# A gated two-layer network on one core: the third main group's routing moved forward in feed-forward 4, the first expert block put inside the last attention's entry, and one shared product moved back

## The chip, the cores and the metric

The kernel runs on one core of a Trainium2 chip. The core has a matrix engine (TensorE, PE in the profile), a vector engine (VectorE, DVE), an activation engine (ScalarE, ACT), GpSimd (POOL), and SyncE (SP), which here only issues transfers. Each engine runs its own queue in order and meets the others at semaphores. The metric is the device time of one execution in microseconds; several executions are taken and their median is given.

## The reference, cut to what matters

x has 16 sequences of 128 tokens of 256 numbers. Four steps are added to it one after the other, each behind a gate:

```
x += tanh(g0) * wkv(layernorm(x), ctx)           # a recurrence over time
x += tanh(g1) * (mlp(layernorm(x)) + experts512)  # feed-forward with 1024 hidden, plus top-8 of 512 tiny experts
x += tanh(g2) * linear_attention(layernorm(x), ctx)
x += tanh(g3) * moe(layernorm(x))
# moe: scores = sigmoid(x @ gate); the two best of 8 experts by scores + bias
for e in range(8):
    out += mask_e * (silu(rin @ w1[e].T) * (rin @ w3[e].T)) @ w2[e].T   # rin = chosen rows, scaled
out = scatter_add(out) + (silu(x @ sw1.T) * (x @ sw3.T)) @ sw2.T        # the shared expert
```

Everything is float32 with the precision that three matmul passes on split operands give in the big products.

## The kernel before, in words

The 16 sequences are four **main groups** of four (0 to 3). Each passes through the recurrence, the feed-forward with its 12 units (eight of the MLP, four of the 512 tiny experts), the attention, and the expert layer. One schedule, written out by hand, sets the order for all engines: `START`, then for each of the four feed-forwards its parts 1 to 13 with the items of `PLAN` behind each part, then `LAST`. Every engine walks the same list (`SCHED`) and issues its own share of each item, so an item's place in the list is its place in each engine's queue. In this text "feed-forward 4" is `("mlp", 3)`.

A part u of a feed-forward issues unit u-1's up products and the down product of unit u-4 (`LAG` is 3). Six banks (`ring`) hold results of TensorE; a bank is opened again once the engine that reads it has freed it.

The expert layer of a main group g is made of these items:

- `moe_in g 0, 1, 2`: part 0 is the statistics on VectorE (L1179 to L1186) and the power that gives 1/sigma on GpSimd (L1601); part 1 the normalisation on VectorE (L1201, writes `xn`); part 2 the transposes on TensorE (L631) and the copy to `xt_f` on ScalarE (L1063). `attn_in` has the same three parts, but ends with a split into a high part `ax_h` (ScalarE, L1059) and a low part `ax_l` (VectorE, L1349).
- `moe g 0`: router scores (TensorE L904), then the choice of two experts per token on VectorE (L1436 to L1458). `moe g 1`: the shared expert's up products (L913, L1106, L1466).
- `place g 0, 1, 2`: counts per expert by a matmul (L923), then the slot of each row on VectorE (L1485 to L1509), then the bookkeeping of which expert owns which block of 128 rows (L1514 to L1529).
- `rows g t`: ScalarE scales tile t twice into buffers (L1118, L1119). `send g t`: GpSimd scatters them into the sorted table `x_rows` in HBM (L1637). It waits for the slots of the group and for the scaled row.
- `load 0 n` and `blk 0 n`: SyncE loads pair n of blocks of the sorted table (L1681); groups 0 to 2 share a first table of 31 blocks, and loads from it start when all their sends have landed. On TensorE `blk n` transposes pair n (L683), does the up products of pair n-1 (L699, after reading the expert numbers into registers), the transposes of the hidden rows of n-2 (L709), and the down products of n-3 (L718). On ScalarE it copies and applies silu (L1131, L1139, L1148, L1156). On VectorE it copies the home indices (L1534) and multiplies (L1543). GpSimd scatters the results of pair n-3 into `y_rows` (L1645).
- `shared g 0`: the shared expert's down product, eight matmuls (L672); `shared g 1`: its addition to x (L1205).
- At the end `fetch`, `gather`, `fetch_tile`, `gather_tile` bring the expert results back and store x.

The loop on VectorE for the home indices reads:

```python
elif kind == "blk":
    for n in range(part + (part > 0), min(part + 2, PAIRS)):
        dve.wait_ge(blocks_loaded[n % 4], 16 * (n // 4 + 1))
        dve.tensor_copy(block_home[:, n, 0:pair_blocks(n)].unsqueeze(2), ...
```

Of the kernel before, what the change touches and what calls it, by code (L numbers as in the profile page):

```python
# [117 lines left out]
def steps(text):  # L118

    out = []  # L120
    for item in text.split(","):
        kind, g, *which = item.split()
        out += [(kind, int(g), int(part)) for part in which]
    return out
# [68 lines left out]
    },  # L193
}

LAST = """mlp_out 3 0, attn_in 3 0, shared 0 0 1, shared 1 0, shared 2 0, attn_in 3 1, shared 1 1, shared 2 1,
    attn_in 3 2, blk 0 0 1, attn 3 0 1 2 3, blk 0 2, attn 3 4 5 6 7, blk 0 3, attn 3 8, blk 0 4, attn 3 9 10, moe_in 3 0,
    blk 0 5, moe_in 3 1, blk 0 6, moe_in 3 2, blk 0 7, moe 3 0, blk 0 8, rows 3 12 13, place 3 0 1, rows 3 14,
    rows 3 15, send 3 12 13 14 15, blk 0 9, place 3 2, blk 0 10 11 12 13 14 15 16 17 18 19 20,
    fetch 0 0 1 2 3 4 5, blk 0 21, gather 0 0, blk 0 22, gather 0 1, blk 0 23, gather 0 2, blk 0 24, gather 0 3, blk 0 25,  # L200
    gather 0 4 5, blk 0 26, moe 3 1, shared 3 0 1, fetch_tile 1 0 1 2 3, gather_tile 1 0 1 2 3"""

# [1 line left out]
for f in range(NG):  # L204

    for part in range(1, MLP_UNITS + 2):
# [5 lines left out]
        if part in PLAN[("mlp", f)]:  # L212
            SCHED += steps(PLAN[("mlp", f)][part])
SCHED += steps(LAST)

# [1610 lines left out]
```

How the kernel before makes its waits and increments, by code:

```python
        def full(eng, key):  # L501
            k, n = place[key]
            eng.wait_ge(bank_full[k], n)
            return ring[k]
# [1 line left out]
        def freed(eng, key):  # L507
            k, n = place[key]
            eng.wait_ge(bank_free[k], n)
# [1 line left out]
        def weigh_values(eng, g, c):  # L512
            ee_a, v = ee_a_of[g], v_of[g]
            eng.wait_ge(ctx_loaded[g], 16 * C)
            freed(eng, (("wkv_in", g), "T", c))
            va = ee_a[c][:, :, :].rearrange("p s (t j) -> p s t j", t=GT)[:, :, :, 1:]
            return eng.tensor_tensor(va[:, 0], va[:, 1], v[c][:, :].rearrange("p (t j) -> p t j", t=GT), ALU.mult)
# [36 lines left out]
        def hidden_made(eng, n):  # L555
            kind, f, u = ALL_UNITS[n]
            if ALL_UNITS[n] in HID_TURN:
                eng.wait_ge(hid_ready, HID_TURN[ALL_UNITS[n]])
            else:
                freed(eng, ((kind, f), "B", u))
# [1 line left out]
        def sent(eng, grp):  # L563
            for k in range(SENDS):
                done = sum(1 for g in range(GROUPS[grp][-1] + 1) for n in range(2 * GT) if (g * 2 * GT + n) % SENDS == k)
                eng.wait_ge(row_sent[k], 16 * done)
# [1 line left out]
        def y_done(eng, n):  # L569
            for k in range(RESULTS):
                blocks = sum(pair_blocks(m) for m in range(k, n, RESULTS))
                if blocks:
                    eng.wait_ge(y_sent[k], 16 * blocks)
# [20 lines left out]
        def xt_wait(eng, n):  # L595
            if n > 0:
                k, turn = place[last_xt_read[n - 1]]
                eng.wait_ge(bank_full[k], turn)
```

## Time and profile before

| | |
|---|---|
| time, median of 3 runs | 522.52 us (520.04 to 523.59) |
| the profiled execution, span from first to last instruction | 517.5 us (its time with what lies around the span isn't listed apart) |
| TensorE busy | 449.8 us, 87% |
| VectorE busy | 360.9 us, 70% |
| ScalarE busy | 246.7 us, 48% |
| GpSimd busy | 154.5 us, 30% |
| mean granted clock of TensorE | 0.967 |

Busy time is a sum over the whole span. Matmuls are pipelined and their ends are modelled, so that starts are the better mark. A granted clock of 1.00 is 2.4 GHz, one of 0.50 is 1.2 GHz. Times in the rows are microseconds from the start of the span.

### The profile page before, as it was taken

Reading aid. Unit: us, or ns where it says so; the run is one execution under the profiler, and the core shown is the slowest. Engines: PE = TensorE matmul, PEld = TensorE weight load, DVE = VectorE, ACT = ScalarE, POOL = GpSimd, SP = SyncE. Lnnn points to the kernel's source line nnn. Section 1 sums busy time; section 2 is a strip of 40 time slices with the busy share of each in tenths; the row PEclk is TensorE's granted clock in tenths of the full one; section 3 lists DMA queues with packets and bytes.
Section 4 is the critical chain, followed back from the end, with each engine's and each line's share of the span. In section 5 each row is a group of like instructions: output and inputs, shape, how many; then the busy total and the mean of one; then the engine's idle time right before and its main releaser. Section 6 shows DMA issues by size and latency. Waiting matters only on the chain. (4 is left out here: it accounts for less than half of the span.)

```text
span 517.5 us, 7233 instructions
## 1 busy us (share of the span) xinstructions
PE 449.8 (87%) x2142; PEld 355.1 (69%) x2142; DVE 360.9 (70%) x1034; ACT 246.7 (48%) x452; POOL 154.5 (30%) x156
## 2 busy tenths in 40 slices
PE   1617999599999889999999999898999799899991
PEld 1315688368578666878778886787777588788851
DVE  6896779995289986565987966978867554531173
ACT  3618574363576346346125315470453454955540
POOL 3955342330002131110000001032336014477771
PEclk9966999799999989999999999999999999999997
DMA  8500312000300000960000000123232423346394
GB/s 303 187 31 30 103 31 83 0 1 0 101 2 0 2 0 14 310 178 0 1 1 1 1 0 2 32 71 102 90 115 83 123 73 91 114 139 208 85 385 153
DMA packets 32965, 42.00 MB, mean 81 GB/s; under 512 B 3483, under 2 KB 26781, under 8 KB 32928
## 3 DMA queue, kind: packets, MB, share of 16 engines
q1 hardware_dynamic: 28224, 32.28, 20.7%
q0 software_dynamic: 3744, 8.42, 4.4%
q10 hardware_dynamic: 960, 0.86, 0.5%
q8 instruction: 18, 0.29, 0.2%
q14 instruction: 19, 0.16, 0.1%
HBM read 24.97 MB, written 18.39 MB: 84 GB/s over the span
## 5 line engine op out<-in xcount | busy, mean ns | idle before, releaser
L660 PE MATMUL acc<-w_down,act_s 128*128 128x256 f32 x384 | 92.2, 387 | 0.9 <-DVE act_s L1386 0.9
L660 PEld LDWEIGHTS acc<-w_down,act_s 128*128 128x128 f32 x384 | 74.6, 195 | 13.2 <-DVE act_s L1386 1.3
L636 PE MATMUL ring<-xt_h,up_l 128*128 128x512 f32 x160 | 70.5, 441 | 2.9 <-DVE xt_l L1356 1.5
L1601 POOL TENSOR_TENSOR rstd<-var_eps,minus_half 128x4 f32<-128x4 f32 x14 | 14.9, 1068 | 176.5 <-DVE var_eps L1186 176.5
L637 PE MATMUL ring<-xt_l,up_h 128*128 128x512 f32 x160 | 63.8, 399 | 0.0
L638 PE MATMUL ring<-xt_h,up_h 128*128 128x512 f32 x160 | 63.7, 398 | 0.0
L1098 ACT ACTIVATE act_s<-ring 128x512 f32<-128x512 f32 x48 | 28.6, 597 | 59.9 <-PE ring L638 59.6
L631 PE MATMUL ring<-small,xn 128*128 128x128 f32 x160 | 23.6, 297 | 26.2 <-ACT xn L998 14.1
L699 PE MATMUL ring<-up_e,act_s 128*128 x184 | 44.3, 383 | 2.3 <-issue 2.0
L1637 POOL DMA_INDIRECT x_rows<-main_a,slots x32 | 31.1, 971 | 43.7 <-ACT main_a L1119 34.8
L1390 DVE TENSOR_TENSOR act_s<-ring,act_s 128x512 f32<-128x512 f32 x32 | 22.0, 686 | 30.8 <-PE ring L638 21.0
L631 PEld LDWEIGHTS ring<-small,xn 128*128 128x128 f32 x160 | 20.1, 153 | 29.6 <-ACT xn L998 14.9
L699 PEld LDWEIGHTS ring<-up_e,act_s 128*128 128x128 f32 x184 | 33.1, 190 | 7.1 <-issue 3.5
L636 PEld LDWEIGHTS ring<-xt_h,up_l 128*128 128x128 f32 x160 | 30.5, 191 | 10.5 <-DVE xt_l L1356 1.8
L638 PEld LDWEIGHTS ring<-xt_h,up_h 128*128 128x128 f32 x160 | 30.5, 191 | 7.3
L637 PEld LDWEIGHTS ring<-xt_l,up_h 128*128 128x128 f32 x160 | 30.6, 191 | 7.0 <-issue 1.4
L1098 ACT ACT_TABLE_LOAD x21 | 26.9, 1283 | 0.4
L1205 DVE SCALAR_TENSOR_TENSOR x_nat<-ring,small,x_nat 128x512 f32<-128x512 f32 x24 | 18.0, 749 | 11.2 <-PE ring L893 7.7
L1179 DVE BATCH_NORM_STATS2 stats<-x_nat 128x6 f32<-128x256 f32 x64 | 22.4, 413 | 4.7 <-DMA x_nat<-in_x 4.3
L1645 POOL DMA_INDIRECT y_rows<-act_s,block_home x16 | 15.9, 994 | 30.3 <-ACT act_s L1156 25.6
L726 PE MATMUL ring<-exps_t_l,sel_exps 128*128 128x512 f32 x24 | 13.5, 564 | 9.9 <-DVE exps_t_l L1361 5.3
L1543 DVE TENSOR_TENSOR pairs<-ring,pairs 128x256 f32<-128x256 f32 x12 | 5.1, 423 | 23.3 <-ACT pairs L1139 23.3
(275 smaller groups left out, 987.8 us busy)
## 6 DMA issues: line engine op xcount, KB each, us to landing
main_b<-x_rows SPq DMA_DIRECT2D x22, 257.0 KB, 2.8
x_rows<-v_t SPq DMA_DIRECT2D x1, 3983.5 KB, 16.7
up_l<-y_rows SPq DMA_DIRECT2D x5, 512.0 KB, 7.0
stage<-in_w_mlp SPq DMA_DIRECT2D x8, 256.0 KB, 2.6
up_e<-in_w_moe SPq DMA_DIRECT2D x8, 256.0 KB, 2.6
x_rows<-v_t SPq DMA_DIRECT2D x1, 1927.5 KB, 22.8
x_nat<-in_x SPq DMA_DIRECT2D x7, 256.0 KB, 7.7
out_x<-x_nat SPq DMA_DIRECT2D x6, 256.0 KB, 5.2
```

Source lines behind the costliest of these rows:

```text
L631: last = pe.transpose(bank[:, t * P:(t + 1) * P], xn[n % 2][:, t, c * P:(c + 1) * P], ident)
L636: pe.matmul(out, wl, xh, start=first, stop=False, skip_group_check=True)
L637: pe.matmul(out, wh, xl, start=False, stop=False, skip_group_check=True)
L638: return pe.matmul(out, wh, xh, start=False, stop=final, skip_group_check=True)
L660: last = pe.matmul(acc[t // 2][:, t % 2, :], act_s[n % RING][:, tok], w_down[:, u, :], start=u == 0 and t % 2 == 0, stop=final, skip_group ...
L699: last = pe.matmul(bank[:, j * 2 * P:(j + 1) * 2 * P], x_block_t[n % 2][:, c, j * P:(j + 1) * P], up_e[:, bass.ds(e * UP + c * 2 * P, 2 * ...
L1098: act.activation(act_s[n % RING][:, :], bank[:, :], ACT.Silu).then_inc(free_sem((step, "A", u)), 1)
L1179: last = dve.bn_stats(stats[:, n, t, :], x_nat[:, b, :])
L1205: return dve.scalar_tensor_tensor(out, bank, gates[:, gate:gate + 1], out, ALU.mult, ALU.add)
L1390: free((step, "B", u), dve.tensor_tensor(s[:, :], bank[:, :], s[:, :], ALU.mult))
L1637: pool.indirect_dma_start(x_rows[group_of(g)], bass.IndirectOffsetOnAxis(ap=slots[:, t, k:k + 1], axis=0), to_send[n % SENDS], None).then_ ...
L1645: pool.indirect_dma_start(y_rows, bass.IndirectOffsetOnAxis(ap=block_home[:, n, j:j + 1], axis=0), y_blocks[n % RESULTS][:, j * D:(j + 1) ...
```

## The change

Only the order of items in the schedule changes; the work is the same. In feed-forward 4 the second and third part of `moe_in 2`, the router and shared up products of group 2 (`moe 2 0 1`) each stand one part earlier; `place 2` stays in part 11, now ahead of the first rows; rows and sends of group 2 are spread over parts 11 and 12 and none are left for part 13. In `LAST`, `blk 0 0` comes between the first and second part of `attn_in 3`, and `shared 2 0` and `shared 2 1` move from there to the place around `blk 0 9`.

```diff
-        8: "attn 2 10, peer_in 3 0, moe_in 2 0, rows 1 4 5, send 1 4 5",
-        9: "moe_in 2 1, rows 1 6, send 1 6",
-        10: "moe_in 2 2, rows 1 7, send 1 7",
-        11: "moe 2 0 1, place 2 0 1 2",
-        12: "rows 2 8 9 10, send 2 8 9 10",
-        13: "mlp 3 14 15, rows 2 11, send 2 11, load 0 0 1 2",
+        8: "attn 2 10, peer_in 3 0, moe_in 2 0, rows 1 4 5, send 1 4 5, moe_in 2 1",
+        9: "moe_in 2 2, rows 1 6, send 1 6",
+        10: "moe 2 0 1, rows 1 7, send 1 7",
+        11: "place 2 0 1 2, rows 2 8 9, send 2 8 9",
+        12: "rows 2 10 11, send 2 10 11",
+        13: "load 0 0 1 2, mlp 3 14 15",
...
-LAST = """mlp_out 3 0, attn_in 3 0, shared 0 0 1, shared 1 0, shared 2 0, attn_in 3 1, shared 1 1, shared 2 1,
-    attn_in 3 2, blk 0 0 1, attn 3 0 1 2 3, blk 0 2, attn 3 4 5 6 7, blk 0 3, attn 3 8, blk 0 4, attn 3 9 10, moe_in 3 0,
+LAST = """mlp_out 3 0, attn_in 3 0, shared 0 0 1, shared 1 0, blk 0 0, attn_in 3 1, shared 1 1, attn_in 3 2, blk 0 1,
+    attn 3 0 1 2 3, blk 0 2, attn 3 4 5 6 7, blk 0 3, attn 3 8, blk 0 4, attn 3 9 10, moe_in 3 0,
...
-    rows 3 15, send 3 12 13 14 15, blk 0 9, place 3 2, blk 0 10 11 12 13 14 15 16 17 18 19 20,
+    rows 3 15, send 3 12 13 14 15, shared 2 0, blk 0 9, place 3 2, shared 2 1, blk 0 10 11 12 13 14 15 16 17 18 19 20,
```

## Rows read from the trace of the kernel before

**Rows 1.** Windows: us, busy PE, PEld, DVE, ACT, POOL (instructions), clock, DMA share, GB/s.
```profile
400.00:410.00 10.00, 6.48 (x35) 4.95 (x34) 7.12 (x16) 3.17 (x6) 0.62 (x1) 1.00 0.53 159
```

**Rows 2.** Waits of TensorE, 396 to 412 us: total us, times, longest.
```profile
PE ring L631 <- DVE xn L1201: 1.2, 1, 1.2
PE ring L699 <- issue: 1.1, 1, 1.1
PE ring L683 <- DMA main_b<-x_rows: 0.9, 1, 0.9
```

**Rows 3.** Chain of waits, 384 to 412 us: start, us, what.
```profile
398.11 2.68 DMA x_rows<-main_a,slots
...
401.92 3.37 DMA main_b<-x_rows
```

**Rows 4.** Timeline, TensorE, 360 to 396: start, us, line, tiles, count [idle before].
```profile
368.90 1.89 PE L660 MATMUL acc<-w_down,act_s 128*128 128x256 f32 x8
...
374.45 1.04 PE L631 MATMUL ring<-small,xn 128*128 128x128 f32 x8
...
380.84 3.68 PE L913 MATMUL ring<-xt_f_pad,stage 128*128 128x512 f32 x8
384.66 0.41 PE L923 MATMUL ring<-wanted,later 128*128 128x32 f32 x2
...
393.99 1.99 PE L660 MATMUL acc<-w_down,act_s 128*128 128x256 f32 x8 [0.86 <-DVE act_s L1386]
```

**Rows 5.** Timeline, VectorE, 368 to 389 us.
```profile
369.33 0.17 DVE L1186 TENSOR_SCALAR var_eps<-mv 128x4 f32<-128x4 f32 x1
...
372.18 1.38 DVE L1201 TENSOR_SCALAR xn<-x_nat,mv,rstd 128x256 f32<-128x256 f32 x4
...
384.44 0.17 DVE L1458 SCALAR_TENSOR_TENSOR row_bias<-row_scale,mv 128x8 f32<-128x8 f32 x1
...
388.80 0.17 DVE L1509 CAST slots<-kv_sum 128x8 uint32<-128x8 f32 x1
```

**Rows 6.** Timeline, GpSimd, 369 to 390 us.
```profile
369.59 1.04 POOL L1601 TENSOR_TENSOR rstd<-var_eps,minus_half 128x4 f32<-128x4 f32 x1 [16.26 <-DVE var_eps L1186]
...
372.17 0.96 POOL L1637 DMA_INDIRECT x_rows<-main_a,slots  x1 [0.30 <-issue]
...
389.25 0.96 POOL L1637 DMA_INDIRECT x_rows<-main_a,slots  x1 [8.52 <-ACT main_a L1119]
```

**Rows 7.** Timeline, VectorE, 400 to 407 us.
```profile
400.97 1.38 DVE L1201 TENSOR_SCALAR xn<-x_nat,mv,rstd 128x256 f32<-128x256 f32 x4
402.27 3.10 DVE L1205 SCALAR_TENSOR_TENSOR x_nat<-ring,small,x_nat 128x512 f32<-128x512 f32 x4
405.40 1.29 DVE L1349 TENSOR_TENSOR ax_l<-ring,ax_h 128x512 fp32r<-128x512 f32 x2
```

**Rows 8.** Timeline, TensorE, 395 to 409: shared down products; first attention matmul.
```profile
395.82 5.34 PE L672 MATMUL ring<-stage,kv_sum 128*128 128x256 f32 x24
...
408.70 0.58 PE L636 MATMUL ring<-ax_h,qg_l 128*128 128x512 f32 x1
```

**Rows 9.** Windows of 1 us in feed-forward 1, columns as in rows 1.
```profile
94.00:95.00 1.00, 0.00 (x0) 0.00 (x0) 1.00 (x1) 0.00 (x0) 0.40 (x1) 0.83 0.00 0
...
101.00:102.00 1.00, 1.00 (x5) 0.86 (x4) 0.96 (x2) 0.00 (x0) 1.00 (x1) 0.76 0.00 0
```

**Rows 10.** Timeline, TensorE, 88 to 103 us.
```profile
96.90 0.76 PE L726 MATMUL ring<-exps_t_l,sel_exps 128*128 128x512 f32 x1 [5.25 <-DVE exps_t_l L1361]
```

**Rows 11.** Timeline, TensorE, 448 to 453: up products of two pairs of blocks.
```profile
448.52 1.99 PE L699 MATMUL ring<-up_e,act_s 128*128 x8 [0.53 <-issue]
...
452.27 1.99 PE L699 MATMUL ring<-up_e,act_s 128*128 x8 [0.24 <-ACT act_s L1131]
```

**Rows 12.** Timeline, GpSimd, near the end: a scatter of results.
```profile
497.58 1.44 POOL L1645 DMA_INDIRECT y_rows<-v_t,block_home  x1 [0.87 <-issue]
```

**Rows 13.** Timeline, ScalarE, near the end: the evacuation it waits for.
```profile
495.95 0.69 ACT L1156 ACTIVATE v_t<-ring,small 128x512 f32<-128x512 f32 x1 [0.51 <-PE ring L718]
```

## The prediction

> **What bounds the kernel now.** I read three views around the seam between feed-forward 4 and the last attention. The windows first: from 400 to 410 us TensorE (PE) is busy for only 6.48 us of ten [rows 1], a hole in a stretch that is otherwise full. The waits name the hole: 1.2 us for the normalised rows of attn_in 3 (written by VectorE, DVE), 0.9 us for the second load of sorted rows, 1.1 us ahead of block 0's up matmuls [rows 2]. The chain of waits says what stands behind the load: the last of main group 2's scatters starts at 398.11 and lands after 2.68 us; then SyncE (SP) issues the loads, and the second lands at 401.92 + 3.37 = 405.29 [rows 3]. So two things arrive there, the attention's rows (402.35) and the blocks (405.3), and the change alters which waits for which.
>
> **Part 1, group 2 sent forward.** The plan moves moe_in 2 1, moe_in 2 2 and moe 2 one part up, and splits the rows and sends of group 2 over parts 11 and 12. What decides when the sends start? The first starts at 389.25 [rows 6], 0.3 after the slots are written (388.80 + 0.17) [rows 5]. The slots follow place's count matmul at 384.66 by 4.3 us of DVE [rows 4]. That matmul is item "place 2 0" of part 11 before and after. I counted what stands ahead of it on PE: the same units, transposes and router and shared matmuls, in another order. PE shows no idle time between 368.90 and it except some 0.14 us behind L913 (380.84 + 3.68 = 384.52), where it waits for the choice of experts, ready at 384.61 [rows 4, 5]. So the sends can come forward by 0.14 us at most: only the label of the part is earlier, not the work. The eight sends follow each other on GpSimd (POOL) without a pause, (398.11 - 389.25) / 7 = 1.27 us each [rows 3, 6], so splitting rows and sends over two parts changes nothing.
>
> The move has a price. The rows of moe_in 2 need stats (var_eps written at 369.50), POOL's power (369.59 to 370.63), then 1.38 us of DVE [rows 5, 6]. Before, unit 8's DVE work filled the wait and PE took the transposes at 374.45, long after the rows. Now they are PE's next item after the down product of 368.90, which ends at 370.79 [rows 4]; the rows are there at 370.63 + 0.1 + 1.38 = 372.1. PE stalls 1.3 us, minus the 0.14 above: place and all behind it are **1.2 us later**. Bounds: 0 if the pipelined ends hide it, 1.5 if PE's free time is 0.2 earlier than its modelled end. ScalarE (ACT) now copies moe_in 2 before it scales rows 6, and rows 7 after moe; both are needed only by POOL sends that ended long before 388.97, so 0. SP's expert loads wait for down products and shift with PE: 0, as the blocks need them only later.
>
> The Trainium skill, page "SBUF — State Buffer", section "SBUF: two separate sides", says that VectorE and GpSimd share one pair of ports under an exclusive lock, the loser waiting out a whole instruction. By that rule the moved normalisation could meet the first send and be held for one send, 0.96 us, and the sum would be 1.0 higher. The trace disagrees: the normalisation at 372.18 runs beside the send at 372.17 in 1.38 us, as the one at 400.97, with no send, does [rows 5 to 7]. I go by the trace.
>
> **Part 2, blk 0 ahead of attn_in 3 1.** PE's part is cheap: four transposes, 0.5 us (half of 1.04 for eight [rows 4]), in time that was idle. But on DVE the item blk 0 copies the home indices of pair 0 *and* pair 1 (lines 1531 to 1534), each behind its load. That wait now stands in front of the normalisation of attn_in 3, and behind that queue shared 1 1, ax_l and the whole attention. Before, the normalisation started at 400.97 [rows 7]; now not before 405.29 + 1.2 = 406.5, plus 0.1 of copies: it ends at **408.0 instead of 402.35**. POOL's power for it is not in the way: it follows the last send, which shifts by the same 1.2.
>
> From that end to the first attention matmul it took 6.35 us (408.70 [rows 8]). Of this the 0.9 wait for the load is gone [rows 2], and block 0's 0.5 of transposes; the 1.1 ahead of the up matmuls may be partly hidden, as PE's sequencer now reads the expert numbers while transposes still run. Upper bound 6.35 - 0.9 - 0.5 = 4.95. Lower bound by DVE: two residual adds (half of 3.10) and ax_l (1.29) [rows 7], 2.85. I take 3.7, between them, as PE itself needs 3.6 for twelve transposes (1.6, at 1.04 for eight) and the first up products (2.0, as at 448.52 [rows 11]). The attention starts at 408.0 + 3.7 = 411.7: **+3.0**, the 1.2 included.
>
> **The clock.** PE's hole grows. Its last shared product used to end at 395.82 + 5.34 = 401.2; with one of three gone (1.8) and the shift it ends at 400.6 [rows 8]. Only block 0's transposes (near 405) lie between that and 408.0. The trace shows what a hole does: after 5.25 us without a matmul, ending at 96.90 [rows 10], the granted clock had gone from 1.00 (2.4 GHz) to half at about 94.7 (0.83 over 94 to 95), 3.0 us after the engine stopped, and came back at 101.5 (0.76 over 101 to 102), 4.6 us after it resumed [rows 9]. Some 2.3 us are lost in 4.6 at half clock. Part of that runs beside the waits for DVE and the sequencer: I take **+1.7**, bounds 0 (the four transposes keep the clock) and 2.3.
>
> **Part 3, shared 2 moved back.** Eight matmuls, 5.34 / 3 = 1.8 us [rows 8], leave a stretch where PE now waits anyway (gain 0), and come in between place 3 0 and blk 9. What covers them there is PE's wait of 0.24 for ACT's copy (452.27) and perhaps the 0.53 ahead of the up matmuls at 448.52 [rows 11]: net 1.3. Behind it PE is full, and the end hangs on it: the pair's result evacuated from 495.95 to 496.64 [rows 13] is scattered from 497.58, with POOL idle 0.87 before it [rows 12]: there POOL waits for PE's result, not PE for POOL. A slightly calmer DMA phase may return 0.3. **+1.0**, bounds 0 (its POOL backlog covers) and 1.8. The residual add, 1.55, lies on DVE, which has idle time there: 0.
>
> **Sum.** 3.0 + 1.7 + 1.0 = +5.7 us. The profiled span is 517.5, some 5.0 below the 522.52 median of the runs; so a span of 523.2 and a time of **528.2 us**.
>
> **Rivals.**
> (B) The DVE wait comes as said, but the clock holds, since block 0's transposes split the hole into 4.4 and 2.5 us, and 3.0 us were needed before 94.7. 3.0 + 1.0: 526.5 us.
> (C) Faster: the sends do leave early. Place would have to finish sooner because DVE has the router's chain behind it when the counts come; for it speaks the 0.9 wait of the last down product for DVE (0.86 at 393.99 [rows 4]), against it the PE order. The point from which it decides: the second load must land by 400.9, 4.4 us sooner. Then the attention starts where DVE allows, 402.35 + 3.7 = 406.0, -2.7; with the 0.86 and part 3's +1.0 the time is 519.9 us. Only with part 3 free and a further gain in the tail would it pass 1%.
> (D) No net effect: stall and wait are half their size and the tail's POOL backlog takes the rest: 523 us.
> (E) Worse: part 3 wholly exposed, clock loss 2.3 and late expert numbers: 4.25 + 2.3 + 1.8 = +8.3, 530.8 us.
>
> **Chances.** Forecast 0.50, B 0.24, C 0.09, D 0.07, E 0.10. About 1%, 5.2 us, is what a measurement of this kernel tells from no change. The forecast lies just beyond it; I give it 0.6 of being slower by over 1%, B 0.15, E all: 0.30 + 0.04 + 0.10 = 0.44. C gives 0.04 of faster; same 0.52. Range: from D's side of B, 522.8, to E, 530.8; this leaves out most of C and the far end of E. The likeliest case alone: 526.8 to 529.8.
>
> **What would show it.** After: DVE waits 4 to 6 us ahead of L1534 just before the normalisation L1201 near 406; first send of group 2 near 390.4, not 385; PE idle over 6 us between 400 and 408 and the granted clock at half near 408; a wait of L631 for xn of 1.3 us near 371; first L636 on ax_h near 413. It is wrong if the sends start before 388, which means that place was not held by PE's order, or if the loads land before the normalisation is due.

## The result, and the profile after

The changed kernel took **530.42 us** in the median of 6 runs (529.81 to 531.29), the kernel before 521.97 us in 6 runs on the same chip (520.04 to 523.76). The ratio is 1.0159, with a 95% interval from 1.0130 to 1.0189: about 8.4 us slower. The forecast was 528.2 us, its range 522.8 to 530.8. The time lies inside the range, 0.4 us from its upper end.

The profiled execution of the changed kernel has a span of 528.8 us, against 517.5 us: 11.3 us more. The two figures differ because the profiled execution of before was a quick one. The runs show a time 1.8 us above the span (530.59 for 528.8), so that 517.5 stands for 519.3 us, 2.7 below the median of before. The 530.59 us stand at the median of after.

I follow the difference along the span by marks that every execution has. The last part of feed-forward 4 before the changed plan acts (L805) starts at 365.16 before and at 365.24 after, so all of it arises behind that mark.

The first shift is the stall in feed-forward 4. TensorE after, 368 to 387 us (start, us, what, idle before):

```profile
369.00 1.89 PE L660 MATMUL acc<-w_down,act_s 128*128 128x256 f32 x8
372.41 1.09 PE L631 MATMUL ring<-small,xn 128*128 128x128 f32 x8 [1.53 <-DVE xn L1201]
...
386.19 0.31 PE L923 MATMUL ring<-wanted,later 128*128 128x32 f32 x2
```

The transposes now follow the down product, and wait 1.53 us for the rows. Place's count stands at 386.19 instead of 384.66 [rows 4], which is 1.5 later. GpSimd after, 390 to 400 us:

```profile
390.53 0.96 POOL L1637 DMA_INDIRECT x_rows<-main_a,slots  x1 [5.48 <-DVE slots L1509]
...
399.35 0.96 POOL L1637 DMA_INDIRECT x_rows<-main_a,slots  x1 [0.30 <-issue]
```

The first send of group 2 starts at 390.53, against 389.25 [rows 6]. The eight follow each other every 1.26 us, against 1.27 before, and the last starts at 399.35, 1.2 later. "Sent forward" moved no send forward.

The second shift is the entry of the attention. VectorE after, 400 to 412 us:

```profile
405.34 0.17 DVE L1534 COPY block_home<-main_b 128x2 uint32<-128x2 uint32 x1 [3.12 <-DMA main_b<-x_rows]
407.04 0.17 DVE L1534 COPY block_home<-main_b 128x2 uint32<-128x2 uint32 x1 [1.53 <-DMA main_b<-x_rows]
407.12 1.38 DVE L1201 TENSOR_SCALAR xn<-x_nat,mv,rstd 128x256 f32<-128x256 f32 x4
...
410.39 1.49 DVE L1349 TENSOR_TENSOR ax_l<-ring,ax_h 128x512 fp32r<-128x512 f32 x2 [0.45 <-ACT ax_h L1059]
```

Two copies of 0.17 us wait 4.65 us for the two loads, and the normalisation behind them starts at 407.12 instead of 400.97 [rows 7]. TensorE after, 397 to 414 us, and the clock of the same time (windows: us, busy PE, PEld, DVE, ACT, POOL, granted clock, DMA share, GB/s):

```profile
397.10 3.62 PE L672 MATMUL ring<-stage,kv_sum 128*128 128x256 f32 x16
405.34 0.91 PE L683 MATMUL ring<-small,main_b 128*128 128x128 f32 x4 [4.62 <-issue]
408.56 1.97 PE L631 MATMUL ring<-small,xn 128*128 128x128 f32 x8 [2.31 <-DVE xn L1201]
...
411.17 2.49 PE L699 MATMUL ring<-up_e,act_s 128*128 x8
413.31 0.58 PE L636 MATMUL ring<-ax_h,qg_l 128*128 128x512 f32 x1
```

```profile
400.00:406.00 6.00, 1.38 (x8) 0.83 (x6) 2.28 (x9) 0.00 (x0) 1.35 (x2) 0.96 0.39 108
406.00:412.00 6.00, 3.69 (x16) 3.29 (x15) 4.33 (x10) 2.38 (x4) 0.00 (x0) 0.50 0.43 135
```

The profile puts the 4.62 us down to "issue", which means that it saw no releaser; but VectorE's copy of the same pair, released by the load, starts in the same moment (405.34), so I read it as the wait for the load. TensorE stands idle for 4.6 and 2.3 us, the clock is at half (1.2 GHz) from 406 to 412, and eight transposes take 1.97 us where eight took 1.04 [rows 4]. The attention starts at 413.31 instead of 408.70 [rows 8], **4.6 us later**. The router scores of group 3 (L904) stand at 445.55 against 440.94: still 4.6, so nothing more is lost between the two.

The third shift is the largest. TensorE after, 445 to 471 us, and its windows:

```profile
445.55 1.85 PE L904 MATMUL ring<-later,xt_f_pad 128*128 128x8 f32 x16
...
451.97 1.97 PE L672 MATMUL ring<-stage,kv_sum 128*128 128x256 f32 x8
453.78 0.60 PE L683 MATMUL ring<-small,main_b 128*128 128x128 f32 x4
454.21 1.89 PE L699 MATMUL ring<-up_e,act_s 128*128 x8
455.94 0.38 PE L709 MATMUL ring<-small,pair_rep 128*128 128x128 f32 x2
456.16 1.03 PE L718 MATMUL ring<-w_down,pair_d 128*128 x4
460.09 1.04 PE L683 MATMUL ring<-small,main_b 128*128 128x128 f32 x4 [2.90 <-DVE x_nat L1205]
461.84 3.78 PE L699 MATMUL ring<-up_e,act_s 128*128 x8 [0.71 <-issue]
...
467.27 0.60 PE L683 MATMUL ring<-small,main_b 128*128 128x128 f32 x4
```

```profile
450.00:460.00 10.00, 6.39 (x34) 5.00 (x32) 7.79 (x44) 7.61 (x23) 4.92 (x6) 1.00 0.31 98
460.00:470.00 10.00, 9.20 (x34) 7.46 (x35) 1.40 (x4) 2.90 (x7) 7.71 (x8) 0.66 0.44 131
```

The same windows of the kernel before:

```profile
450.00:460.00 10.00, 9.76 (x55) 8.32 (x54) 4.58 (x23) 7.38 (x18) 6.64 (x7) 1.00 0.49 160
460.00:470.00 10.00, 10.00 (x56) 8.72 (x55) 1.61 (x6) 5.29 (x12) 7.55 (x9) 1.00 0.53 167
```

`shared 2 0` (L672) writes two of the six banks. The four steps of `blk 9` behind it take the other four, so the transposes of `blk 10` want the first of the two again, six openings on. They wait 2.90 us for the addition that reads it. What VectorE did meanwhile, with the slots, the bookkeeping of `place 3 2` and the addition (450 to 461 us, after):

```profile
455.69 0.17 DVE L1509 CAST slots<-kv_sum 128x8 uint32<-128x8 f32 x1
...
457.45 0.16 DVE L1514 SCALAR_TENSOR_TENSOR room<-pages,over 128x8 f32<-128x8 f32 x1
...
459.19 1.54 DVE L1205 SCALAR_TENSOR_TENSOR x_nat<-ring,small,x_nat 128x512 f32<-128x512 f32 x2
```

The addition belongs to `shared 2 1`, which the list puts behind `place 3 2`. Then the clock falls: the up products of 1.9 us take 3.78. The transposes of `blk 11` start at 467.27; before they started at 455.18. That is 12.1 later, against 4.6 at the router scores: 7.5 us in one stretch of twenty. The last scatter of results starts at 517.70 instead of 506.54, 11.2 later. So 0.9 came back on the way to the end. Before, GpSimd had scatters waiting near 472 us and sent one every 1.29 us; after, it waits for results there. GpSimd before, then after:

```profile
472.02 0.99 POOL L1645 DMA_INDIRECT y_rows<-kv_sum,block_home  x1 [0.30 <-issue]
```

```profile
472.24 0.98 POOL L1645 DMA_INDIRECT y_rows<-v_t,block_home  x1 [0.96 <-ACT v_t L1156]
```

In sums along the profiled span: 4.6 up to the attention, 6.6 from there to the last scatter, 0.1 behind it. The forecast had 4.7 and 1.0.

### The profile page after: what moved, and what is told of

The parts are those of the page before. It is cut to its first block and busy times, and to the rows that moved or that the text cites. A ratio compares the mean times of both kernels' runs of the same rounds, so it can differ in the third digit from the quotient of the medians.

```text
span 528.8 us, 7226 instructions
## 1 busy us (share of the span) xinstructions
PE 454.0 (86%) x2134; PEld 358.9 (68%) x2142; DVE 361.0 (68%) x1034; ACT 246.8 (47%) x452; POOL 153.9 (29%) x156
## 5 line engine op out<-in xcount | busy, mean ns | idle before, releaser
L699 PE MATMUL ring<-up_e,act_s 128*128 x184 | 46.3, 396 | 1.2 <-issue 1.2
L699 PEld LDWEIGHTS ring<-up_e,act_s 128*128 128x128 f32 x184 | 34.8, 199 | 5.9 <-issue 1.8
L1205 DVE SCALAR_TENSOR_TENSOR x_nat<-ring,small,x_nat 128x512 f32<-128x512 f32 x24 | 18.0, 748 | 11.2 <-PE ring L893 7.7
L1131 ACT ACTIVATE act_s<-ring 128x512 f32<-128x512 f32 (+1 forms) x24 | 13.8, 574 | 24.0 <-PE ring L683 24.0
```

The lines of the kernel that those rows point to most:

```text
L699: last = pe.matmul(bank[:, j * 2 * P:(j + 1) * 2 * P], x_block_t[n % 2][:, c, j * P:(j + 1) * P], up_e[:, bass.ds(e * UP + c * 2 * P, 2 * ...
L1205: return dve.scalar_tensor_tensor(out, bank, gates[:, gate:gate + 1], out, ALU.mult, ALU.add)
```

## The experiments

Each ratio is to the kernel before in runs on the same chip, with its 95% interval. Where a trace is read, I name its L805 mark, because that mark moves by up to 2 us between executions of code that is the same up to there. "Net of the marks" means less the difference of the two marks.

**The plan of feed-forward 4 alone** (the kernel before with only the `PLAN` lines of the change).

```diff
-        8: "attn 2 10, peer_in 3 0, moe_in 2 0, rows 1 4 5, send 1 4 5",
+        8: "attn 2 10, peer_in 3 0, moe_in 2 0, rows 1 4 5, send 1 4 5, moe_in 2 1",
...
-        13: "mlp 3 14 15, rows 2 11, send 2 11, load 0 0 1 2",
+        13: "load 0 0 1 2, mlp 3 14 15",
```

> Only part 1: the kernel before with the new parts 8 to 13 of feed-forward 4, LAST untouched. Theory (sends are bound by PE's order, so only the stall of the transposes L631 is added): PE waits about 1.5 us near 371, place's L923 starts at 386.2 instead of 384.7, the first send of group 2 near 390.5, the loads and the attention 1.5 later: +1.3 to +1.6 us. Rival (the move costs nothing by itself, the 8.4 us come from LAST): 0 within 0.5 us. Rival that the move gains: -1 us or more.

Measured: 523.35 us, ratio 1.0048 (1.0031 to 1.0064), some 2.5 us slower. The stall is there, but the price is twice what the prediction took it for, and above the 1.3 to 1.6 expected here. The loads come later: the transposes of pair 1 wait 1.17 us for theirs and start at 407.22, against 405.33 before. TensorE and the clock behind that (L805 at 365.55):

```profile
408.96 3.54 PE L699 MATMUL ring<-up_e,act_s 128*128 x8 [1.08 <-issue]
411.94 0.93 PE L636 MATMUL ring<-ax_h,qg_l 128*128 128x512 f32 x1
```

```profile
408.00:412.00 4.00, 3.04 (x9) 2.42 (x9) 0.55 (x4) 0.52 (x1) 0.00 (x0) 0.66 0.47 134
```

The four waits between the last shared product and block 0's up products add up to 3.8 us instead of 3.5, and the clock has fallen at their end: the up products need 3.54 us. In the profile of before it held at 1.00 there [rows 1]. That is one execution of each. Over all runs the mean granted clock of the span is hardly lower: 0.958 to 0.965 in the twelve of this kernel (mean 0.9609), 0.956 to 0.967 in the seventeen of before (0.9616). So it is not shown that the clock makes up the difference between 1.3 and 2.5 us.

**Block 0 alone** (only `blk 0 0` moved ahead of `attn_in 3 1`).

```diff
-LAST = """... shared 2 0, attn_in 3 1, shared 1 1, shared 2 1,
-    attn_in 3 2, blk 0 0 1, ...
+LAST = """... shared 2 0, blk 0 0, attn_in 3 1, shared 1 1, shared 2 1,
+    attn_in 3 2, blk 0 1, ...
```

> Only part 2: the kernel before with blk 0 0 ahead of attn_in 3 1, shared 2 left where it was. Theory (VectorE's home copies wait for the second load ahead of the normalisation): normalisation starts near 405.4 instead of 401.0, first attention matmul near 410.6 if the clock holds (+1.9) and 412 if it falls (+3.3); the whole kernel +2 to +3.5 us. Rival (the wait is covered by the loads that TensorE waited for anyway): 0 to +0.5 us.

Measured: 525.87 us, ratio 1.0087 (1.0069 to 1.0105). The wait of VectorE is 4.8 us in two pieces, and the clock is at 0.50 from 408 to 412. With L805 at 365.21 the attention starts at 414.07, 5.4 later than before. The direction is as expected, and the size above the 2 to 3.5 us. Of the 2.1 us by which the attention is later than the 412 expected with a fallen clock, 0.7 lie ahead of the normalisation, which starts at 406.08 instead of 405.4 because the second load came later; 1.4 lie behind it, at half clock. The clock stays low behind the start of the attention too (0.55 from 412 to 416).

**The third shared product alone** (only `shared 2 0` and `shared 2 1` moved back).

```diff
-LAST = """... shared 2 0, attn_in 3 1, shared 1 1, shared 2 1,
+LAST = """... attn_in 3 1, shared 1 1,
...
-    rows 3 15, send 3 12 13 14 15, blk 0 9, place 3 2, blk 0 10 ...
+    rows 3 15, send 3 12 13 14 15, shared 2 0, blk 0 9, place 3 2, shared 2 1, blk 0 10 ...
```

> Only part 3: the kernel before with shared 2 0 ahead of blk 9 and shared 2 1 behind place 3 2. Theory from the trace of the changed kernel (the two banks of shared 2 stay full until VectorE has done place 3 2, so blk 10's transposes wait 2.9 us, and the clock falls behind that wait): a wait of L683 of 2.5 to 3 us near 455, clock at half for some 4 us behind it, +5 to +6.7 us. Rival, the prediction's own: only 1.0 us, +0 to +1.8.

Measured: 528.06 us, ratio 1.0135 (1.0112 to 1.0157), some 7.0 us slower: the dearest single part, and the one that the prediction had priced at 1.0. TensorE and windows of this kernel:

```profile
457.12 0.63 PE L683 MATMUL ring<-small,main_b 128*128 128x128 f32 x4 [2.90 <-DVE x_nat L1205]
458.87 3.77 PE L699 MATMUL ring<-up_e,act_s 128*128 x8 [1.12 <-issue]
```

```profile
455.00:460.00 5.00, 1.75 (x7) 1.37 (x8) 2.72 (x9) 0.60 (x1) 3.78 (x5) 0.79 0.42 100
460.00:465.00 5.00, 5.00 (x17) 3.89 (x16) 0.50 (x2) 0.95 (x3) 3.78 (x5) 0.53 0.43 149
```

The same wait of 2.90 us and the same half clock appear without parts 1 and 2. Net of the marks (366.67 here, 365.16 before) the attention and the router scores start 0.1 us later than before, the last scatter 7.0 later (515.07): all of it arises behind the router scores. The Trainium skill, page "TensorE: Matmul & The Clock Gate", section "🎯 Why this matters for your kernels", says that idle gaps between bursts of matmuls send the engine back to its lower clock; by that rule the wait costs more than its own length, and the trace agrees (0.53 from 460 to 465, where the kernel before has 1.00), after a gap that is a little shorter than those which the page warns of.

By themselves the three parts cost 2.5, 4.5 and 7.0 us, 14.0 in sum; together they cost 8.4. The difference lies at the entry of the attention. Net of the marks it starts 2.9 us late with the plan alone, 5.3 with block 0 alone, 0.1 with the shared product alone, and 4.5 with all three. The plan alone and block 0 alone both show a fall of the clock there in their profiles, and the changed kernel has it once; and with the third product gone, VectorE has one addition fewer ahead of `ax_l` (1.53 us at 408.42 instead of 3.10 at 407.38 with block 0 alone).

**The changed kernel with the banks freed early** (`shared 2 1` directly behind `shared 2 0`, all else as changed). It was run twice, on two chips.

```diff
-    rows 3 15, send 3 12 13 14 15, shared 2 0, blk 0 9, place 3 2, shared 2 1, blk 0 10 ...
+    rows 3 15, send 3 12 13 14 15, shared 2 0 1, blk 0 9, place 3 2, blk 0 10 ...
```

> The changed kernel with one item moved: shared 2 1 directly behind shared 2 0, so that VectorE frees the two banks before blk 9. If the held banks cost what the trace says (2.9 us of waiting, 2.4 of half clock), it is 4.5 to 5.5 us faster than the changed kernel, near 525.3 us, +3 to +4 against before. If they cost nothing: 530.4.

> The changed kernel with shared 2 1 directly behind shared 2 0, a second time, as the base for the kernel with short filler products that runs on the same chip. The bank theory expects 4.3 to 4.9 us less than the changed kernel again, a ratio of 1.007 to 1.010 to the kernel before.

Measured: 525.79 us, ratio 1.0083 (1.0064 to 1.0102), and 525.50 us, ratio 1.0087 (1.0059 to 1.0116). One word moved in the list returns 0.7 of the 1.6%: 1.0159 / 1.0085 = 1.0073, or 3.8 us (4.6 and 4.9 in the bare medians, which were not taken on one chip). The first run had been expected 4.5 to 5.5 below the changed kernel and 3 to 4 above before; it is 4.8 above. The second lies in its expected ratio of 1.007 to 1.010. No transpose waits for the addition now, and the clock stays at 1.00 from 440 to 510. The second profile has its L805 mark at 365.27, like after and before, and so compares directly: attention at 413.10 (after 413.31), router scores at 445.40 (445.55), last scatter at 512.20 (517.70). The place of `shared 2 1` alone is worth 5.5 us in the profiled executions. What stays of part 3 is (512.20 - 506.54) - (445.40 - 440.94) = 1.2 us.

**The home copies behind the normalisation** (the kernel with free banks, and the copies of pairs 0 and 1 done in item `blk 1`).

```diff
-                    for n in range(part + (part > 0), min(part + 2, PAIRS)):
+                    for n in range((part + 1) * (part > 1), min(part + 2, PAIRS) * (part > 0)):
```

> The kernel a_free_banks, but VectorE copies the home indices of pairs 0 and 1 in item blk 1, not in blk 0, so that no load stands ahead of the normalisation of attn_in 3; TensorE's transposes of block 0 stay ahead of those of attn_in 3. Theory (the wait on VectorE is what part 2 costs): normalisation near 402.5 instead of 407, TensorE then waits only for the first load (near 405.3), attention 2.5 to 4 us earlier than in a_free_banks, the kernel 2.5 to 4 us faster, near 522.5. Rival (the wait of TensorE for load 0 ahead of attn_in's transposes is the cost): no gain over 1 us.

Measured: 522.98 us, ratio 1.0027 (1.0002 to 1.0052), against 1.0083 without this edit on another chip: 2.9 us returned. VectorE and TensorE of this kernel (L805 at 364.99):

```profile
402.01 1.38 DVE L1201 TENSOR_SCALAR xn<-x_nat,mv,rstd 128x256 f32<-128x256 f32 x4
```

```profile
404.94 0.87 PE L683 MATMUL ring<-small,main_b 128*128 128x128 f32 x4 [4.47 <-issue]
...
410.69 0.58 PE L636 MATMUL ring<-ax_h,qg_l 128*128 128x512 f32 x1
```

The rows were there at 403.4, and now TensorE's own wait, which I again read as that for the load, stands in front of them. The clock still fell, to 0.65 over 404 to 408. So the wait was moved from VectorE to TensorE. The kernel stays some 1.4 us slower than before (0.1 to 2.7 by the interval), and in this profile the attention still starts 2.2 later than before, net of the marks.

**Filler products that hold the clock** (the kernel with free banks; products into an accumulator whose results are not used, ahead of and behind block 0's transposes).

```diff
+                        for _ in range(9):
+                            pe.matmul(acc[0][:, 0, :], wo[:, 0, 0:P], wo[:, 0, :], start=True, stop=True)
                     if n < PAIRS:
                         transpose_blocks(n)
+                    if n == 0:
+                        for _ in range(4):
+                            pe.matmul(acc[0][:, 0, :], wo[:, 0, 0:P], wo[:, 0, :], start=True, stop=True)
```

> The kernel a_free_banks with 28 extra matmuls of 128x256 on TensorE into a bank that nothing reads any more: 18 ahead of block 0's transposes (3.9 us in the wait for the load) and 10 behind them (2.2 us in the wait for the normalised rows). Work is added, none taken away. Theory (the hole lets the clock fall and that costs 1.5 to 2 us): granted clock 1.00 from 400 to 416, the first attention matmul 1.5 to 2 us earlier, the kernel 1.5 to 2 us faster than a_free_banks. Rival (the clock is no part of it, only the wait): the same time as a_free_banks, or up to 1 us more if the fillers overrun the waits.

> As a_fill with half the fillers (9 and 4 products, each of which is two matmul instructions of 0.22 us: 3.9 and 1.7 us), so that they end before the load and the normalised rows arrive. Theory (the fall of the clock in the hole costs time of its own): granted clock 1.00 from 400 to 416, the first attention matmul 1.5 to 2 us sooner than in a_free_banks, the kernel 1.5 to 2 us faster, near 524. Rival: same as a_free_banks, 525.8.

> The same kernel with 9 and 4 filler products ahead of and behind block 0's transposes, which hold the granted clock at 1.00 through the wait; the results of the fillers are not used. If the fall of the clock at 408 to 412 us costs the median what one profiled execution showed (about 1.9 us), the ratio is 0.003 to 0.004 below that of the kernel without fillers on this chip. If the executions without fillers lose the clock less often or at other places, so that the median hides it, the two ratios are within 0.0015 of each other, as on two different chips before.

The first form had 18 and 10 such products. Each became two instructions, the first group took 7.93 us and delayed block 0 itself: 527.73 us, ratio 1.0121 (1.0091 to 1.0152), slower than without. That expectation failed by my miscount: the clock held at 1.00 from 396 to 420, but the run can't say what that is worth. The short form (the diff) gave 524.25 us, ratio 1.0086 (1.0062 to 1.0109), and on the chip of the second base 524.03 us, ratio 1.0067 (1.0041 to 1.0093), against 1.0087 there without fillers. TensorE and windows of the second one (L805 at 365.45; lines behind the inserted ones stand six further down, so that L1207 is L1201 of the others):

```profile
400.79 4.05 PE L935 MATMUL acc<-wo 128*128 128x256 f32 x18
405.50 0.66 PE L683 MATMUL ring<-small,main_b 128*128 128x128 f32 x4 [0.66 <-DMA main_b<-x_rows]
405.99 1.89 PE L940 MATMUL acc<-wo 128*128 128x256 f32 x8
409.07 1.09 PE L631 MATMUL ring<-small,xn 128*128 128x128 f32 x8 [1.19 <-DVE xn L1207]
...
412.58 0.58 PE L636 MATMUL ring<-ax_h,qg_l 128*128 128x512 f32 x1
```

```profile
408.00:412.00 4.00, 2.59 (x17) 2.25 (x18) 3.78 (x9) 1.57 (x3) 0.00 (x0) 1.00 0.24 80
```

The clock holds at 1.00, although the load and the normalised rows come no sooner. The other executions agree: the mean granted clock of the span is 0.961 to 0.965 in the six runs with fillers and 0.953 to 0.959 in the six without on this chip. The spans are 523.6 without and 522.3 with fillers. In the medians the gain is 1.5 us in this pair; in the other, on two chips, the ratios show none, and the intervals overlap. **How much the front's fall of the clock costs in the median stays open between 0 and about 2 us.**

**Sending earlier in earnest** (the kernel with free banks, and the shared up products of group 2 moved behind place, so that its counts come sooner).

```diff
-        10: "moe 2 0 1, rows 1 7, send 1 7",
-        11: "place 2 0 1 2, rows 2 8 9, send 2 8 9",
+        10: "moe 2 0, rows 1 7, send 1 7",
+        11: "place 2 0 1 2, moe 2 1, rows 2 8 9, send 2 8 9",
```

> The kernel a_free_banks with the shared up products of group 2 (moe 2 1, 3.4 us of TensorE) behind place 2 instead of ahead of it. Theory (TensorE's order ahead of place sets when the sends of group 2 start, and their last landing sets the attention in the changed kernel): L923 near 382.6 instead of 386.2, first send near 387.7 instead of 390.5, second load landed 2.7 us sooner, the kernel 2.7 to 4 us faster than a_free_banks, 521.8 to 523. Rival (the sends wait for something else, or the attention does): the same as a_free_banks within 0.7 us.

Measured: 524.78 us, ratio 1.0099 (1.0073 to 1.0125). No gain over 1.0083 to 1.0087 can be seen. The first send did start at 388.60 instead of 390.55, but the last only 1.5 sooner (397.85 for 399.39 in the second run with free banks), and the clock fell sooner as well:

```profile
404.00:408.00 4.00, 2.18 (x11) 1.78 (x10) 2.87 (x7) 1.11 (x2) 0.00 (x0) 0.50 0.67 201
408.00:412.00 4.00, 4.00 (x14) 3.37 (x13) 1.46 (x3) 1.27 (x3) 0.00 (x0) 0.50 0.23 66
```

Eight microseconds at half clock lie behind it, and the attention starts at 412.00, 1.1 sooner than in the second run with free banks. My expectation of 2.7 to 4 us treated the clock as fixed; it was not.

**Attention ahead of the blocks** (the kernel before with four items of the attention ahead of `blk 0 0 1`, and `shared 2 1` behind `attn_in 3 2`).

```diff
-    attn_in 3 2, blk 0 0 1, attn 3 0 1 2 3, blk 0 2, attn 3 4 5 6 7, blk 0 3, ...
+    attn_in 3 2, shared 2 1, attn 3 0 1 2 3, blk 0 0 1, attn 3 4 5 6 7, blk 0 2 3, ...
```

> From the kernel before: the attention's projections ahead of all blocks (attn 3 0 1 2 3, blk 0 0 1, attn 3 4 5 6 7, blk 0 2 3), and shared 2 1 behind attn_in 3 2. Theory (TensorE's hole before is the wait for the second load and the expert numbers): first attention matmul near 405.6 instead of 408.7 with three block steps still to do, net gain 0.7 to 1.2 us against before, more in executions where the clock falls in the hole. Rival: ScalarE's tables and the later blocks give it back, 0 to +1 us.

Measured: 521.47 us, ratio 0.9991 (0.9969 to 1.0013), no difference, where a gain of 0.7 to 1.2 us was expected. The attention starts at 406.11 (L805 at 366.04), but the clock falls there:

```profile
403.30 1.09 PE L631 MATMUL ring<-small,xn 128*128 128x128 f32 x8 [1.24 <-DVE xn L1201]
406.11 0.48 PE L636 MATMUL ring<-ax_h,qg_l 128*128 128x512 f32 x1 [1.72 <-DVE ax_l L1349]
```

```profile
408.00:412.00 4.00, 4.00 (x15) 3.22 (x14) 0.84 (x2) 2.17 (x4) 0.00 (x0) 0.75 0.00 0
```

It falls once more in this execution, far behind the edit, where the same waits of 0.80 and 0.53 us left it at 1.00 in the kernel before (there the same products took 1.99 us [rows 11]):

```profile
450.40 3.25 PE L699 MATMUL ring<-up_e,act_s 128*128 x8 [0.53 <-issue]
```

**Only block 0's transposes in the gap** (the kernel before; `blk 0 0` stays directly behind `attn_in 3 2`, `shared 2 1` comes behind it, and `blk 0 1`, whose up products wait for the sequencer, goes behind four items of the attention).

```diff
-    attn_in 3 2, blk 0 0 1, attn 3 0 1 2 3, blk 0 2, attn 3 4 5 6 7, blk 0 3, ...
+    attn_in 3 2, blk 0 0, shared 2 1, attn 3 0 1 2 3, blk 0 1 2, attn 3 4 5 6 7, blk 0 3, ...
```

> As b_attn_first, but block 0's transposes ahead of the attention's projections and blocks 1 and 2 behind them. Theory: the transposes fill 0.4 us of the wait for ax_l, so 1.0 to 1.5 us faster than before. Rival: VectorE's home copies of blk 0 wait for the second load ahead of shared 2 1, whose banks the projections need: no better than b_attn_first.

Measured: **518.39 us** (517.91 to 520.18), ratio 0.9948 (0.9926 to 0.9971): faster than the kernel before by an interval clear of 1, and so than the changed one (1.0130 to 1.0189). TensorE and windows (L805 at 365.40):

```profile
402.66 1.09 PE L631 MATMUL ring<-small,xn 128*128 128x128 f32 x8 [1.24 <-DVE xn L1201]
404.16 0.63 PE L683 MATMUL ring<-small,main_b 128*128 128x128 f32 x4 [0.41 <-issue]
405.48 0.47 PE L636 MATMUL ring<-ax_h,qg_l 128*128 128x512 f32 x1 [0.69 <-DVE ax_l L1349]
```

```profile
408.00:412.00 4.00, 4.00 (x21) 3.28 (x20) 1.47 (x3) 2.37 (x5) 0.00 (x0) 1.00 0.01 2
```

The 0.63 us of transposes stand where TensorE waited for `ax_l`, and the attention starts 3.2 us sooner than before. It gained 3.0 us where 1.0 to 1.5 were expected. The two kernels that begin the attention near 406 differ by 0.0043 in the ratio, and the clock differs with them: the mean of the span is 0.958 over the twelve runs of the first and 0.962 over the ten of this one. That block 0's transposes in the gap are what holds the clock is not shown, as the places of `blk 0 1` and `blk 0 2` differ too.

## Why the prediction was right, and where it was not

**Part 1, the plan.** "The sends can come forward by 0.14 us at most": right. The stall was sized 1.2 with an upper bound of 1.5, and measured 1.5 at place's count and 1.2 to 1.3 at the sends. The port lock that the Trainium skill states (page "SBUF — State Buffer", section "SBUF: two separate sides") was priced at 0.96 us and left out of the sum. The normalisation at 370.82 ran beside the send at 370.91 in 1.54 us instead of 1.38, so it was not held for a whole send. This does not refute the page, as the prediction had it: the page ties the lock to instructions of VectorE in a two-port mode, or with two inputs in SBUF against a GpSimd instruction that reads SBUF, and no row shows that this one is of either kind. What was missed is that part 1 alone costs some 2.5 us and not 1.2; the clock fell in its one profile, and whether that is the rest is open.

**Part 2, block 0 first.** Right in mechanism. The wait of VectorE in front of L1534 was forecast at 4 to 6 us and measured 4.65; the end of the normalisation at 408.0 and measured at 408.50 (407.12 + 1.38); the start of the attention at 411.7 plus 1.7 for the clock, 413.4, and measured 413.31. Rival B, in which the clock holds, is out: four transposes did not keep it. The close agreement of 413.4 and 413.31 is in part luck. The second load was due at 406.5 and came at 407.02, since the last scatter took 2.99 us instead of 2.68 and the load 3.54 instead of 3.37; the way from the end of the normalisation to the attention was due to take 5.4 and took 4.8. Putting the copies behind the normalisation returned 2.9 us of the 4.5 that block 0 alone costs, which shows the wait as the cause of over half of this part.

**The clock at the front.** Taken as +1.7 with bounds 0 and 2.3. The trace shows the fall. With fillers the spans, net of the marks, say 1.5 and 2.3 (523.6 to 522.3, the marks 0.18 apart; and 525.3 to 521.2, less the 1.84 by which the marks differ), the medians 1.5 and 0. It is within the bounds, and not settled.

**Part 3, the failed term.** The prediction said +1.0, "bounds 0 and 1.8". It measured 6.6 us in the profiled execution, 7.0 as the only edit (in the profile and in the medians). The step that failed is "The residual add, 1.55, lies on DVE, which has idle time there: 0". The idle time was counted, not the place in the queue. The addition stands behind `place 3 2`; until it has run, two of six banks are held, and TensorE is stopped when the ring comes round. The product itself was sized well: with the banks free, 1.2 us of part 3 are left, against the forecast 1.0. The kernel with one item moved shows both. Its move returned 3.8 us by the ratios and 5.5 in the profiles; no run here explains the 1.7 between them.

**The sum.** In profiled spans, 5.7 were forecast and 11.3 measured; the 5.6 between them are part 3's. In medians, 528.2 against 530.42 is off by only 2.2. This smaller miss owes something to a second error. The prediction carried the 5.0 us between the span of before and its median over to after in full; but after's executions lie close together (529.81 to 531.29), and their median is 1.6 above the profiled span. The profiled execution of before was a quick one, with a mean granted clock of 0.967, the upper end of what the runs of that kernel show (0.956 to 0.968); that others lose the clock at 400 to 410 is likely, but no other was profiled. The two errors, some 5.6 too little and 3.4 too much, make up the 2.2, so that the time fell so near the forecast by luck. The range held it, but the reason for a result near its top was not rival E, "part 3 wholly exposed" at 1.8: it was a wait that no case contained.

## What to carry to other kernels

When a step is moved in an in-order schedule with a ring of buffers, count two distances: from its write to the next use of the same buffer, and from its write to its reader on the reader's queue. If the reader stands behind other work, the ring stops the writer, however idle the reader's engine is on average. A copy that waits for a transfer belongs behind everything on its queue that could run without it. A gap on TensorE is priced with the half clock that may follow it, and such a price is a chance and not a constant. The order with 0.63 us of real transposes in a gap gained 3.0 us; how much of this is the held clock is not shown.

## What the runs showed of the hardware

- **The same short gaps may or may not cost the clock.** Waits of 1.24 and 1.72 us with 1.09 us of transposes between them were followed by a clock of 0.75 over 408 to 412 (attention ahead of the blocks); waits of 1.24, 0.41 and 0.69 were not (1.00). But neither were the 1.24, 0.29, 0.92 and 1.07 us of the kernel before (1.00 from 400 to 412), while 1.25, 0.29, 1.17 and 1.08 us were with the plan alone (0.66 over 408 to 412). Waits of 0.80 and 0.53 us were followed by 0.66 over 450 to 455 in one execution and by 1.00 in the other. So neither the longest wait nor their sum decides it in these traces. A wait of 2.90 us was followed by half clock both times it occurred (0.66 over 460 to 470 after the change, 0.53 over 460 to 465 with the shared product alone).
- **The same code differs by up to 2 us before any edit acts.** The L805 mark lay between 364.99 and 367.04 in fourteen executions, one of each kernel run. It goes with the clock in the hole of feed-forward 1: the windows of 93 to 96 and 102 to 104 us show 0.78 and 1.00 in the kernel before, and 1.00 and 0.78 in the kernel with only the shared product moved (mark at 366.67). The medians of before in five sets of runs were 519.61 to 521.97. A single profile is compared only net of such a mark.
- **One fp32 product of 128x256 is two instructions here:** nine filler products were 18 instructions in 4.05 us, 18 were 36 in 7.93 us.
